# A float32 output projection becomes three float32r products, and moves one step later

## The chip, the cores and the metric

The kernel runs on one core of a Trainium2 chip. The metric is the device time of one execution in microseconds (us); lower is better. TensorE is PE in the profile, VectorE is DVE, ScalarE is ACT, GpSimd is POOL, SyncE (which issues the DMAs) is SP. The change touches only how one small matrix product is fed and when it runs.

## The reference, cut to what matters

Four attention layers follow each other on `x` (2048 x 256) with a context of 1601 x 512. Layers 0, 2 and 3 ("wide": 16 heads of 64) compute

```
q = x @ Wq;  k = ctx @ Wk;  v = ctx @ Wv          # 16 heads of 64
probs = softmax(q @ k.T / 8 + column bias)        # 2048 x 1601 per head
out = probs @ v                                   # 2048 x 1024, heads side by side
x = out @ Wo + bo + x                             # Wo: 1024 x 256
```

Layer 1 has 16 heads of 16 and an RMS norm; the change leaves it alone. The change is in `out @ Wo`: the product of the normalised attention output with `Wo`, added to the residual.

## The kernel before, in words

**Heads and steps.** A wide head is cut into 7 steps (`STEPS`) of two key tiles of 128 (the last has one). In a step the PE first runs 8 units, then multiplies the two tiles of exponentials with `V` (`values`, the L968 rows, float32, into banks OA and OB). A unit is one 128 x 512 score tile as two float32r products (`scores`, L957 and L958, into one of three ST banks) and one or two 400-wide score tiles for the row maximum of the next head (`s_tile`, L938, into one of three SS banks). ACT turns each ST bank into exponentials `P` (`exps`). DVE takes the maximum of each SS bank (`s_max`).

**Row sums.** The 13 tiles of exponentials of a head are added up in `acc`: tiles 0 to 2 on DVE (`add`, the first as 0 + 1, L1520, at the end of step 0; the second, L1526, at the end of step 1), tiles 3 to 12 on POOL (L838, two instructions a tile). POOL's first add of a head waits for DVE's second one, and its last adds of a head run into step 0 of the next head. In a layer's last head POOL has tiles 3 and 4 only, and DVE the others up to tile 10. Between its adds for tiles 7 to 10 POOL does four divisions (`divide`, L817), which write the normalised output of the head before into `On`.

**Output projection.** Two heads make a pair: `On` is 128 x 2048 (two heads of 64 rows), and `Wo`'s part of a pair is 128 x 256. A pair is projected in 8 items (`output`, L1003): item i gives 128 output columns by 512 rows of x; j = i // 2 says which 512 columns of `On` it reads. An item is one float32 product, which the trace shows as two MATMUL records. It takes an SS bank out of the same ring of three that `s_tile` uses (`wait_ring`: the bank must have been drained), and DVE adds it to the residual (`add_output`, L1546, or L1543 for a layer's first pair). `o_item` places the items: in steps 0 and 1 of odd heads from head 3 on, in every second unit. So 7 pairs of each layer go out inside heads 3, 5, ..., 15, and the eighth pair after the last head (`end`). `wo` has two buffers, loaded by SP at the end of odd heads.

**What sets the order.** Every engine runs a list written out in the program, in order. Semaphores with constant targets couple the lists. Instructions behind a waiting one wait too. The order of SS banks comes from `ring_order`, which PE, DVE and ACT all follow.

**Names the change touches.** `o_item`, `output`, `load_wo` and its calls in SP's `head`, `q_phase` and `group_layer`, the allocation of `On`, `wo` and `sel`, and the `head` functions of POOL, ACT and DVE.

Of the kernel before, what the change touches and what calls it, by code (L numbers as in the profile page):

```python
# [207 lines left out]
def attention_layers(nc, a):  # L208
    with ExitStack() as ctx:
# [15 lines left out]
        sel = at("sel", [128, 128], o + 1024)  # L225
# [46 lines left out]
        On = at("On", [128, NQ], o)  # L272
        o += 8192
# [4 lines left out]
        R = at("R", [128, 2, 512], o + 8192)  # L278
        o += 12288
        wo = [at(f"wo{b}", [128, C], o + 1024 * b) for b in range(2)]  # L280
        o += 2048

# [79 lines left out]
        d_wq, d_wo, d_m = sem("d_wq"), [sem(f"d_wo{b}") for b in range(2)], sem("d_m")  # L362
# [100 lines left out]
        def r_spread(H):  # L463

            return 128 * (H + 1 - (H + 1) // HEADS)

# [7 lines left out]
        def _(sp):  # L474
# [131 lines left out]
            def load_wo(n):  # L606
                sp.dma_start(wo[n % 2][:, :], a["wo"][n, :, :]).then_inc(d_wo[n % 2], 16)
# [15 lines left out]
            def q_phase(l):  # L623
# [38 lines left out]
                if l == 0:  # L662
                    load_v(1)
                    for n in range(2):
                        load_wo(n)
                if l == 2:
                    sp.wait_ge(pe_o, 8 * n0)
                    load_wo(n0 + 1)
# [64 lines left out]
            def group_layer():  # L733
# [10 lines left out]
                for h in range(HEADS):  # L744
# [12 lines left out]
                    if h == HEADS - 3:  # L757
# [3 lines left out]
                        for n in range(PAIRS, PAIRS + 2):  # L761
                            load_v(n)
                            load_wo(n)
# [30 lines left out]
        def _(gp):  # L794
# [24 lines left out]

            def head(H):  # L820
                first = adds_before(pool_tiles, H)
                for t in range(3, KT):
# [7 lines left out]
                    for c in range(2):  # L830
# [7 lines left out]
                        gp.tensor_tensor(out, out, P[0:k, slot(H, t), q, :], ALU.add).then_inc(pool_a, 1)  # L838

# [35 lines left out]
        def _(pe):  # L875
# [120 lines left out]
            def output(n, i):  # L996
                at, ct, j = RING_AT["o", n, i], i % CT, i // CT
                if i == 0:
                    pe.wait_ge(d_wo[n % 2], 16 * (n // 2 + 1))
# [3 lines left out]
                pe.matmul(SS[at % 3][:, :], wo[n % 2][:, ct * 128:(ct + 1) * 128], On[:, j * 512:(j + 1) * 512],  # L1003
# [31 lines left out]
            def head(l, h):  # L1035
                H = l * HEADS + h
                for g in range(STEPS):
                    for u, (on, t, j) in enumerate(units(h, g)):
# [3 lines left out]
                        if o_item(h, g, u) is not None:  # L1042
                            output(l * PAIRS + (h - 3) // 2, o_item(h, g, u))
# [11 lines left out]
            def end(l):  # L1055
                for i in range(8):
                    output(l * PAIRS + PAIRS - 1, i)
# [124 lines left out]
        def _(act):  # L1182
# [102 lines left out]

            def take_z(H):
# [36 lines left out]
            def head(l, h):  # L1323
                H = l * HEADS + h
                for g in range(STEPS):
                    if takes_sums(h, g - 1):
                        take_z(H - 1)
                    for on, t, j in units(h, g):
                        if j == 0:
                            exps(H + on, t)  # L1330
# [425 lines left out]
```

## Time and profile before

| | |
|---|---|
| time, median of 3 runs | 4620.56 us (4617.27 to 4621.11) |
| profiled execution | 4619.93 us |
| its span, first to last instruction | 4618.1 us |
| PE busy | 4523.6 us (98%) |
| DVE busy | 2989.6 us (65%) |
| POOL busy | 2674.4 us (58%) |
| ACT busy | 2262.0 us (49%) |
| granted PE clock, mean of the span | 0.987 of full speed |

The span is what the profile covers; 1.8 us of the execution's own time lie around it. A matmul's reported duration overlaps its neighbours, so the cost of one is read from the start of one row to the start of the next. A timeline row has start, duration, engine, line, operation, output and inputs, the count of merged instructions, and in brackets the idle time before it with its releaser. Where a row stands for several instructions, its duration is from the first one's start to the last one's end.

### The profile page before, as it was taken

To read this page: it belongs to the slowest core of one execution; us is meant where nothing else is said; L and a number is where in the kernel's file an instruction comes from. 1 tells how busy PE (TensorE), PEld (TensorE's weight loads), DVE (VectorE), ACT (ScalarE), POOL (GpSimd) and SP (SyncE) were. 2 spreads that over 40 slices of the span, in tenths; PEclk is the share of its full clock that TensorE was granted. 3 is DMA by queue.
4 is the path that set the end of the run, shared out by engine and by line. 5 is a ranking of instruction groups with operands and counts; after the bars stand their busy time and mean duration, and the time that the engine had idled before them with its cause. 6 is when DMAs were issued, how large, how long until landed. Compare 5 with 4: busy or idle time off the path is not lost.

```text
span 4618.1 us, 56243 instructions
## 1 busy us (share of the span) xinstructions
PE 4523.6 (98%) x20489; PEld 2807.1 (61%) x20489; DVE 2989.6 (65%) x5016; ACT 2262.0 (49%) x4016; POOL 2674.4 (58%) x1281
## 2 busy tenths in 40 slices
PE   8999999999999979999999999999999999999999
PEld 7888865555556545555556555555556655565554
DVE  3321467667766678778746667766767667676766
ACT  3222454454445436666655444444455545454443
POOL 0000367797778611111036887788774877788775
PEclk9999999999999979999999999999999999999999
DMA  4555832221222021011233221222216212222220
GB/s 151 178 188 163 289 79 64 66 68 45 66 64 52 12 39 16 12 15 16 58 109 111 67 67 45 64 68 52 52 46 221 63 39 64 64 68 54 58 48 28
DMA packets 124629, 349.64 MB, mean 76 GB/s; under 512 B 28085, under 2 KB 46005, under 8 KB 113338
## 3 DMA queue, kind: packets, MB, share of 16 engines
q1 hardware_dynamic: 124352, 346.04, 28.4%
q8 instruction: 162, 2.65, 0.3%
q14 instruction: 115, 0.94, 0.1%
HBM read 191.31 MB, written 120.31 MB: 67 GB/s over the span
## 4 chain that ended last, share of the span: by engine, by line
PE 95%; DVE 3%; DMA 1%; issue 1%; SPq 0%; ACT 0%; POOL 0%; DVEq 0%; ACTq 0%
PE ST L957 14%; PE SS L938 13%; PE ST L958 13%; PE OA L968 12%; PE OB L968 11%; PE ST L1090 5%; PE OA L1098 4%; PE SS L1003 4%; PE SS L1076 3%; PE OB L1076 1%; PE SS L977 1%; PE ST L1021 1%; PE ST L1022 1%; PE ST L1023 1%; DVE mpart L1599 1%; PE SS L925 1%
## 5 line engine op out<-in xcount | busy, mean ns | idle before, releaser
L838 POOL TENSOR_TENSOR acc<-acc,P 128x1024 f32<-128x1024 f32 x912 | 2203.2, 2448 | 598.4 <-DVE acc L1526 585.3
L1277 ACT ACTIVATE P<-ST 128x512 f32<-128x512 f32 (+1 forms) x2496 | 1465.4, 598 | 1305.4 <-PE ST L958 1169.8
L1499 DVE TENSOR_REDUCE mpart<-SS 128x1 f32<-128x400 f32 (+1 forms) x3072 | 1627.8, 569 | 676.2 <-PE SS L938 600.4
L938 PE MATMUL SS<-KS,QS 68*128 68x400 f32 (+1 forms) x3072 | 1037.9, 371 | 11.1 <-DMA QS<-stq 8.3
L957 PE MATMUL ST<-QX,KX 128*128 128x512 f32 (+1 forms) x2496 | 1032.9, 414 | 3.6 <-DMA QS<-mrow 2.0
L958 PE MATMUL ST<-QS,KS 69*128 69x512 f32 (+1 forms) x2496 | 989.0, 396 | 0.0
L938 PEld LDWEIGHTS SS<-KS,QS 68*128 68x128 f32 x3072 | 583.9, 190 | 222.6 <-DVE mpart L1499 33.5
L957 PEld LDWEIGHTS ST<-QX,KX 128*128 128x128 f32 (+1 forms) x2496 | 463.0, 185 | 389.2 <-issue 287.6
L968 PE MATMUL OA<-P,Vp 128*64 128x512 f32 (+1 forms) x2496 | 658.3, 606 | 0.0
L968 PE MATMUL OB<-P,Vp 128*64 128x512 f32 (+1 forms) x2496 | 641.3, 592 | 0.0
L1359 ACT ACTIVATE PG<-ST 128x512 f32<-128x512 f32 (+1 forms) x832 | 426.2, 616 | 213.3 <-PE ST L1090 213.0
L958 PEld LDWEIGHTS ST<-QS,KS 69*128 69x128 f32 (+1 forms) x2496 | 464.4, 186 | 14.7 <-issue 5.8
L847 POOL TENSOR_TENSOR On<-Oraw,Z 32x512 f32<-32x512 f32 x64 | 81.7, 1277 | 663.6 <-ACT Z L1184 660.0
L1599 DVE TENSOR_REDUCE mpart<-SS 128x1 f32<-128x400 f32 (+1 forms) x768 | 396.2, 563 | 83.0 <-PE SS L1076 83.0
L865 POOL TENSOR_TENSOR stq<-stw,stq 128x512 fp32r<-128x512 f32 x96 | 123.1, 1289 | 521.4 <-ACT stw L1184 519.7
L968 PEld LDWEIGHTS OB<-P,Vp 128*64 128x64 f32 (+1 forms) x2496 | 179.1, 137 | 356.6 <-issue 356.6
L968 PEld LDWEIGHTS OA<-P,Vp 128*64 128x64 f32 (+1 forms) x2496 | 149.3, 136 | 268.0 <-issue 181.8
L817 POOL TENSOR_TENSOR On<-Oraw,R 64x512 f32<-64x512 f32 x192 | 252.5, 1315 | 91.4 <-issue 40.2
L1546 DVE TENSOR_TENSOR xacc<-SS,xacc 128x512 f32<-128x512 f32 x168 | 115.7, 690 | 174.4 <-PE SS L1003 174.4
L1003 PE MATMUL SS<-On,wo 128*128 128x512 f32 x384 | 197.9, 605 | 9.0 <-issue 9.0
L1098 PE MATMUL OA<-PG,Vg 128*32 128x512 f32 (+1 forms) x1664 | 201.5, 599 | 0.0
L1526 DVE TENSOR_TENSOR acc<-acc,P 128x1024 f32<-128x1024 f32 x132 | 172.1, 1351 | 21.0 <-POOL acc L838 14.0
(240 smaller groups left out, 4206.4 us busy)
## 6 DMA issues: line engine op xcount, KB each, us to landing
q_parts<-stq SPq DMA_DIRECT2D x96, 512.0 KB, 5.4
QX<-q_parts SPq DMA_DIRECT2D x96, 512.0 KB, 11.3
KX<-k_parts SPq DMA_DIRECT2D x48, 801.0 KB, 9.2
QS<-q_parts SPq DMA_DIRECT2D x45, 512.0 KB
R<-R SPq DMA_DIRECT2D x360, 64.0 KB, 2.0
v_tiles<-sv SPq DMA_DIRECT2D x24, 832.0 KB, 6.4
Vp<-v_tiles SPq DMA_DIRECT2D x24, 832.0 KB, 7.2
k_parts<-skh SPq DMA_DIRECT2D x48, 400.5 KB, 4.9
```

What stands on the lines that cost most here:

```text
L817: gp.tensor_tensor(On[64 * e:64 * e + 64, j * 512:(j + 1) * 512], Oraw[r, c, :], R[r, c, :], ALU.mult)\
L838: gp.tensor_tensor(out, out, P[0:k, slot(H, t), q, :], ALU.add).then_inc(pool_a, 1)
L938: pe.matmul(SS[at % 3][:, 0:w], QS[H % 3][0:SROWS, qt * 128:(qt + 1) * 128], KS[H % 3][0:SROWS, o:o + w], start=True, stop=True).then_inc( ...
L957: pe.matmul(bank, KX[H % 2][:, t * 128:t * 128 + k], QX[H % 2][:, q], start=True, stop=False)
L958: pe.matmul(bank, KS[H % 3][0:MXROW + 1, t * 128:t * 128 + k], QS[H % 3][0:MXROW + 1, q], start=False, stop=True).then_inc(pe_st, 1)
L968: last = pe.matmul(OAB[j // 2][r:r + 64, :], Vp[n % 2][0:k, t, 64 * e:64 * e + 64], P[0:k, slot(H, t), j, :], start=t == 0, stop=t == KT - 1)
L1003: pe.matmul(SS[at % 3][:, :], wo[n % 2][:, ct * 128:(ct + 1) * 128], On[:, j * 512:(j + 1) * 512], start=True, stop=True).then_inc(pe_o, 1)
L1098: last = pe.matmul(OA[j * QD:j * QD + QD, :], Vg[0:k, t, g * QD:g * QD + QD], PG[slot(h, t) * JQ + j][0:k, :], start=t == 0, stop=t == KT - 1)
L1277: act.activation(P[0:k, slot(H, t), j, :], ST[n % 3][0:k, :], ACT.Exp, scale=SCALE).then_inc(act_p, 1)
L1359: act.activation(PG[slot(h, t) * JQ + j][0:k, :], ST[n % 3][0:k, :], ACT.Exp, scale=SCALE1).then_inc(gact_p, 1)
L1499: dve.tensor_reduce(mpart[H % 2][:, i // len(KCH), c:c + 1], SS[RING_AT["s", H, i] % 3][:, 0:w], AX.X, ALU.max).then_inc(dve_ss, 1)
L1599: dve.tensor_reduce(mpart[h % 2][:, i // len(KCH), c:c + 1], GS[GRING_AT["s", h, i] % 4][:, 0:w], AX.X, ALU.max).then_inc(gdve_ss, 1)
```

## The change

Inside the heads the float32 product becomes three float32r products that sum into one bank: hi weights by hi output, hi weights by lo output, lo weights by hi output. The last pair of a layer keeps the float32 product (`last_output`). Four new kinds of instruction make the parts:

- ACT copies `wo` to `woh` (128 x 256) after step 4 of the even head in which a pair's division runs, and DVE subtracts to get `wol`, right behind the maximum of the next head;
- ACT copies `On` to `Onh` in four pieces of 128 x 512: j = 0, 1 at the end of that even head, j = 2, 3 after step 1 of the odd head that follows (`Onh` has room for two pieces);
- POOL subtracts to get `Onl` (in place of `On`): j = 0, 1 behind its last add of the even head, j = 2, 3 in front of its first add of the odd head;
- an item's PE wait is now for `wol` (item 0) and for its piece of `Onl` (items 0, 2, 4, 6).

The items move from steps 0 and 1 to steps 1 and 2. `wo` has one buffer, and SP loads it behind the spreading of the reciprocals of the odd head instead of at its end. `sel`, used in layer 1 only, moves into an unused part of `R`.

```diff
 def o_item(h, g, u):
-    if h % 2 == 1 and h >= 3 and g < 2 and u % 2 == 0:
-        return 4 * g + u // 2
+    if h % 2 == 1 and h >= 3 and 1 <= g < 3 and u % 2 == 0:
+        return 4 * (g - 1) + u // 2
     return None
+def pair_ended(l, h):
+    return l * PAIRS + (h - 2) // 2 if h % 2 == 0 and h >= 2 else None
+def pair_going_out(l, h):
+    return l * PAIRS + (h - 3) // 2 if h % 2 == 1 and h >= 3 else None
...
# SP, head(l, h)
                 if h > 0:
                     spread(H - 1)
+                if pair_going_out(l, h) is not None:
+                    sp.wait_ge(pe_o, 8 * (pair_going_out(l, h) + 1))
+                    load_wo(pair_going_out(l, h) + 1)
...
-                if h % 2 == 1 and h >= 3 and H + 2 < end:
-                    sp.wait_ge(pe_o, 8 * (H // 2))
-                    load_wo(H // 2 + 1)
...
# POOL
+            def output_lo(n, j):
+                q = slice(j * 512, (j + 1) * 512)
+                gp.wait_ge(act_onh, 4 * split_before(n) + j + 1)
+                gp.tensor_tensor(Onl[:, q], On[:, q], words(Onh[:, j % 2, :]), ALU.subtract).then_inc(pool_onl, 1)
             def head(H):
+                if pair_going_out(l, h) is not None:
+                    for j in range(2, JQ):
+                        output_lo(pair_going_out(l, h), j)
                 for t in range(3, KT):
...
+                if pair_ended(l, h) is not None:
+                    for j in range(2):
+                        output_lo(pair_ended(l, h), j)
...
# PE, output(n, i)
                 if i == 0:
-                    pe.wait_ge(d_wo[n % 2], 16 * (n // 2 + 1))
+                    pe.wait_ge(dve_wol, split_before(n) + 1)
+                if ct == 0:
+                    pe.wait_ge(pool_onl, 4 * split_before(n) + j + 1)
+                wait_ring(pe, at)
+                pe.matmul(SS[at % 3][:, :], woh[:, w], Onh[:, j % 2, :], start=True, stop=False)
+                pe.matmul(SS[at % 3][:, :], woh[:, w], Onl[:, q], start=False, stop=False)
+                pe.matmul(SS[at % 3][:, :], wol[:, w], Onh[:, j % 2, :], start=False, stop=True).then_inc(pe_o, 1)
...
# ACT
+            def output_hi(n, j):
+                act.wait_ge(pool_on, 4 * (2 * n + 1) + j + 1)
+                wait(act, pe_o, 8 * n + 2 * j - 2)
+                copy(Onh[:, j % 2, :], On[:, j * 512:(j + 1) * 512]).then_inc(act_onh, 1)
+            def weights_hi(n):
+                act.wait_ge(d_wo, 16 * (n + 1))
+                copy(woh[:, :], wo[:, :]).then_inc(act_woh, 1)
...
# DVE
+            def weights_lo(n):
+                dve.wait_ge(act_woh, split_before(n) + 1)
+                dve.tensor_tensor(wol[:, :], wo[:, :], words(woh[:, :]), ALU.subtract).then_inc(dve_wol, 1)
...
+                    if g == 4 and pair_ended(l, h) is not None:
+                        weights_lo(pair_ended(l, h))
```

On POOL, at the turn from head 2 to head 3 of the first layer (`acc` is one head's sum, `Oraw` the raw output that is divided), the program before has these rows:

```order
L838 TENSOR_TENSOR acc_112<-acc_112,P 128x1024 x4
L838 TENSOR_TENSOR acc_112<-acc_112,P 65x1024 x2
L838 TENSOR_TENSOR acc_113<-acc_113,P 128x1024 x8
L817 TENSOR_TENSOR On<-Oraw,R 64x512
L838 TENSOR_TENSOR acc_113<-acc_113,P 128x1024 x2
```

The changed program has at the same place, on POOL:

```order
L867 TENSOR_TENSOR acc_111<-acc_111,P 128x1024 x4
L867 TENSOR_TENSOR acc_111<-acc_111,P 65x1024 x2
L844 TENSOR_TENSOR Onl<-On,Onh 128x512 x4
L867 TENSOR_TENSOR acc_112<-acc_112,P 128x1024 x8
L838 TENSOR_TENSOR On<-Oraw,R 64x512
```

The four subtractions stand between the last add of one head (65 rows high) and the first of the next; two of them belong to the one head and two to the other.

On DVE, in steps 0 and 1 of the same head 3 (`mpart<-SS` are row maxima, `xacc` the residual), the program before has:

```order
L1543 SCALAR_TENSOR_TENSOR xacc<-SS,bo,xacc 128x512
L1499 TENSOR_REDUCE mpart_52<-SS 128x1 x2
L1520 TENSOR_TENSOR acc_113<-P 128x1024 x2
L1543 SCALAR_TENSOR_TENSOR xacc<-SS,bo,xacc 128x512
L1499 TENSOR_REDUCE mpart_52<-SS 128x1 x3
```

The changed program has around the same adds on DVE, from the end of head 2 on:

```order
L1566 TENSOR_REDUCE negm<-mpart_52 128x16
L1591 TENSOR_TENSOR wol<-wo,woh 128x256
L1571 CAST mrow<-SS 16x128
L1560 TENSOR_REDUCE mpart_51<-SS 128x1 x24
L1581 TENSOR_TENSOR acc_112<-P 128x1024 x2
L1608 SCALAR_TENSOR_TENSOR xacc<-SS,bo,xacc 128x512
L1560 TENSOR_REDUCE mpart_51<-SS 128x1 x3
```

No item is left in front of DVE's first two adds of the odd head (`acc<-P`), and `wol` stands in front of the row of maxima.

On PE, behind the V products of head 2's last step (L1000 in the changed program, step 0's are the 128x512 rows of OA and OB), the changed program's first item reads:

```order
L989 MATMUL ST<-QX_68,KX_75 128x512
L990 MATMUL ST<-QS_64,KS_69 128x512
L1036 MATMUL SS<-Onh,woh 128x512
L1037 MATMUL SS<-Onl,woh 128x512
L1038 MATMUL SS<-Onh,wol 128x512
L970 MATMUL SS<-KS_70,QS_65 128x402
```

The three products stand where one L1003 row stood, behind the score tile of a unit.

## Rows read from the trace of the kernel before

**Rows 1.** The page: busy share of PE, and the chain that ended last.
```profile
PE 4523.6 (98%) x20489; PEld 2807.1 (61%) x20489; DVE 2989.6 (65%) x5016; ACT 2262.0 (49%) x4016; POOL 2674.4 (58%) x1281
...
PE 95%; DVE 3%; DMA 1%; issue 1%; SPq 0%; ACT 0%; POOL 0%; DVEq 0%; ACTq 0%
```

**Rows 2.** Timeline of PE, one unit with an item and one without, head 5.
```profile
903.10 1.02 PE L1003 MATMUL SS<-On,wo 128*128 128x512 f32 x2
...
904.14 0.39 PE L957 MATMUL ST<-QX,KX 128*128 128x512 f32 x1
...
904.61 0.35 PE L938 MATMUL SS<-KS,QS 68*128 68x400 f32 x1
904.79 0.39 PE L957 MATMUL ST<-QX,KX 128*128 128x512 f32 x1
```

**Rows 3.** Timeline of PE, three float32r products of 512 columns, V projection.
```profile
449.71 0.40 PE L925 MATMUL ST<-wvh,ch 128*128 128x512 f32 x1
...
450.41 0.39 PE L925 MATMUL ST<-wvh,ch 128*128 128x512 f32 x1
```

**Rows 4.** Timeline of PE, first layer: starts of steps in heads 5 and 6.
```profile
899.97 0.50 PE L957 MATMUL ST<-QX,KX 128*128 128x512 f32 x1
...
913.19 0.51 PE L957 MATMUL ST<-QX,KX 128*128 128x512 f32 x1
...
913.77 1.02 PE L1003 MATMUL SS<-On,wo 128*128 128x512 f32 x2
...
969.63 0.50 PE L957 MATMUL ST<-QX,KX 128*128 128x512 f32 x1
...
979.01 0.50 PE L957 MATMUL ST<-QX,KX 128*128 128x512 f32 x1
```

**Rows 5.** Timeline of POOL, its last add before head 5's own.
```profile
906.23 2.37 POOL L838 TENSOR_TENSOR acc<-acc,P 65x1024 f32<-65x1024 f32 x1
```

**Rows 6.** Timelines of POOL and DVE, their adds in step 0 of head 6.
```profile
973.93 5.70 POOL L838 TENSOR_TENSOR acc<-acc,P 65x1024 f32<-65x1024 f32 x2
...
976.03 1.39 DVE L1520 TENSOR_TENSOR acc<-P 128x1024 f32<-128x1024 f32 x1
...
977.34 3.37 DVE L1520 TENSOR_TENSOR acc<-P 128x1024 f32<-128x1024 f32 x1
```

**Rows 7.** Timelines of POOL and DVE, divisions beside adds, second wide layer's last head.
```profile
3471.57 2.05 POOL L817 TENSOR_TENSOR On<-Oraw,R 64x512 f32<-64x512 f32 x1 [0.17 <-POOL On L817]
3473.78 2.05 POOL L817 TENSOR_TENSOR On<-Oraw,R 64x512 f32<-64x512 f32 x1 [0.17 <-POOL On L817]
...
3472.40 2.29 DVE L1526 TENSOR_TENSOR acc<-acc,P 128x1024 f32<-128x1024 f32 x1
```

**Rows 8.** All instructions by line: POOL's subtraction of 128 x 512.
```profile
L865 POOL TENSOR_TENSOR stq<-stw,stq 128x512 fp32r<-128x512 f32 x96 | 123.1, 1289 | 521.4 <-ACT stw L1184 519.7
```

**Rows 9.** Timelines of PE, POOL and DVE, head 15 of the first layer.
```profile
1557.14 0.50 PE L957 MATMUL ST<-QX,KX 128*128 128x512 f32 x1
...
1568.11 0.50 PE L957 MATMUL ST<-QX,KX 128*128 128x512 f32 x1
...
1610.58 1.02 PE L989 MATMUL SS<-acc,ones 128*64 128x512 f32 x2
...
1554.13 15.00 POOL L838 TENSOR_TENSOR acc<-acc,P 128x1024 f32<-128x1024 f32 x6
...
1564.77 5.44 DVE L1520 TENSOR_TENSOR acc<-P 128x1024 f32<-128x1024 f32 x2
...
1592.71 15.71 DVE L1526 TENSOR_TENSOR acc<-acc,P 128x1024 f32<-128x1024 f32 x10
```

**Rows 10.** Busy time and granted clock by stretch (PEclk: third from the end); PE timeline.
```profile
203.00:209.00 6.00, 3.56 (x10) 2.60 (x9) 4.94 (x6) 1.84 (x4) 0.00 (x0) 0.73 0.97 318
279.00:285.00 6.00, 3.56 (x16) 2.79 (x16) 2.15 (x4) 2.11 (x5) 0.00 (x0) 1.00 0.81 266
...
572.00:577.00 5.00, 2.98 (x13) 1.78 (x12) 0.00 (x0) 3.03 (x7) 2.84 (x3) 1.00 1.05 408
...
205.89 0.80 PE L925 MATMUL SS<-wvh,ch 128*128 128x512 f32 x1 [2.44 <-DVE wvl L1424]
```

More of the change, by code:

```diff
@@ L272, in attention_layers @@
         On = at("On", [128, NQ], o)
+        Onl = at("Onl", [128, NQ], o, F32R)
         o += 8192
@@ L278, in attention_layers @@
         R = at("R", [128, 2, 512], o + 8192)
+        sel = at("sel", [128, 128], o + 8192 + 1024)
         o += 12288
-        wo = [at(f"wo{b}", [128, C], o + 1024 * b) for b in range(2)]
+        wo = at("wo", [128, C], o)
+        wol = at("wol", [128, C], o, F32R)
+        woh = at("woh", [128, C], o + 1024, F32R)
         o += 2048
+        Onh = at("Onh", [128, 2, 512], o, F32R)
+        o += 4096
         o = main
@@ L359, in attention_layers @@
         dve_bias, dve_tok, dve_ext = sem("dve_bias"), sem("dve_tok"), sem("dve_ext")
-        d_wq, d_wo, d_m = sem("d_wq"), [sem(f"d_wo{b}") for b in range(2)], sem("d_m")
+        d_wq, d_wo, d_m = sem("d_wq"), sem("d_wo"), sem("d_m")
+        act_woh, dve_wol, act_onh, pool_onl = sem("act_woh"), sem("dve_wol"), sem("act_onh"), sem("pool_onl")
         d_s = [sem(f"d_s{b}") for b in range(3)]
@@ L465, in r_spread, with split_before @@
             return 128 * (H + 1 - (H + 1) // HEADS)
+        def split_before(n):
+            return n - n // PAIRS
         def q_stored(l, q):
@@ L663, in q_phase @@
                     load_v(1)
-                    for n in range(2):
-                        load_wo(n)
+                    load_wo(0)
                 if l == 2:
                     sp.wait_ge(pe_o, 8 * n0)
-                    load_wo(n0 + 1)
+                    load_wo(n0)
             def head(l, h):
@@ L762, in group_layer @@
                             load_v(n)
-                            load_wo(n)
+                        load_wo(PAIRS)
                     sp.wait_ge(gpe_st, (h + 1) * HU)
@@ L1056, in end @@
                 for i in range(8):
-                    output(l * PAIRS + PAIRS - 1, i)
+                    last_output(l * PAIRS + PAIRS - 1, i)
             def group_project(rnd, j):
@@ L1330, in head @@
                             exps(H + on, t)
+                    if g == 1 and pair_going_out(l, h) is not None:
+                        for j in range(2, JQ):
+                            output_hi(pair_going_out(l, h), j)
+                    if g == 4 and pair_ended(l, h) is not None:
+                        weights_hi(pair_ended(l, h))
+                if pair_ended(l, h) is not None:
+                    for j in range(2):
+                        output_hi(pair_ended(l, h), j)
                 if h == 0:
@@ L1580, in head @@
                         reciprocals(H - 1)
+                    if g == 4 and pair_ended(l, h) is not None:
+                        weights_lo(pair_ended(l, h))
             def end(l):
```

17 lines of the change are left out of this document (11 added, 6 removed).

## The prediction

> **What bounds the kernel now.** I read the page first: PE is busy for 98% of the span and carries 95% of the chain that ended last [rows 1]. So any time taken off the PE's list inside the heads is time off the span, as long as PE never has to wait; and any new wait of PE is paid in full. Then I read PE's timeline in a head with items and in one without, always from start to start. An item's rows begin at 903.10 and the next unit's first product at 904.14; of these 1.04 us the 400-wide tile in between takes 0.18 (904.61 to 904.79), so one float32 item costs PE 0.86 us [rows 2]. A step without items lasts 9.38 us (969.63 to 979.01), one with four items 13.22 (899.97 to 913.19) [rows 4]: 3.84 for four items, of which 3.44 are the items themselves and 0.4 are short waits for an SS bank. Last I read POOL and DVE around the turn of the heads, because the changed items wait for POOL. All times there are from T, the start of a head's first score product behind the V products of the head before.
>
> **The product itself.** 168 items lie in the heads (7 pairs x 8 items x 3 layers). Three float32r products of 512 columns take 0.70 us from start to start (449.71 to 450.41, each with its own weight load) [rows 3]. That is 0.16 less than 0.86, and 168 x 0.16 = 26.9 us off. The bounds: 0.14 to 0.17 an item, 23 to 29 us. The section "TensorE Precision Notes" of the page FP8 and Floating Point Precision of the Trainium skill says that true float32 takes four passes and reduced float32 one; by that ratio three products would cost three quarters of 0.86, and the sum would be some 9 us lower. The rows show 0.70 and not 0.645, so I stay with 0.16. PE's four fewer items in step 0 and four more in step 2 cancel but for the waits priced below.
>
> **The wait that the change adds.** Item 0 of an odd head waits for Onl's first piece, and the whole of PE's list stands behind it: scores, maxima, V products, and with them ACT and DVE. When is that piece ready?
>
> Item 0 is now in step 1. Step 0 has lost its items and lasts 9.38 like that of an even head; the item comes 0.58 later (913.19 to 913.77) [rows 4]. So PE is there at T + 9.96.
>
> POOL's last add of the head before runs from 906.23 to 908.60, that is T + 6.26 to T + 8.63 [rows 5], and `output_lo` stands behind it. A POOL subtraction of 128 x 512 takes 1.29 us [rows 8]. With nothing else the piece would be ready at T + 9.9, just in time. Two things come in between.
>
> First, DVE. In head 5 DVE's two first adds came behind step 0's items. Without them DVE does what it does in even heads: its first add starts at 976.03, T + 6.40, and it collides with POOL. In head 6 two POOL adds take 5.70 us and not 2 x 2.37, the second DVE add takes 3.37 and ends at T + 11.08 [rows 6, 5]. Each waits for the other's whole instruction. In [rows 7] the two engines take turns: a POOL instruction of 512 columns starts every 2.21 us, of which DVE's 1024 columns fill 1.07 (from the end of POOL's at 3473.62 to DVE's own end at 3474.69) and POOL's own work 1.14.
>
> Second, the new `wol` subtraction on DVE in step 4 of the even head, 128 x 256. One 1024-column DVE add held POOL up by 5.70 - 4.74 = 0.96 us [rows 5, 6], so a quarter of the columns should cost it 0.24 to 0.3. POOL has no idle time from there to the end of the head's adds, so the shift stays. The trace has no such small DVE instruction beside POOL; the bounds are 0 (it does not collide) and 0.96 (it does like a whole add). I take 0.27. The section "Who interferes with whom" of the page SBUF — State Buffer of the Trainium skill says that a tensor_tensor with both inputs in SBUF contends with GpSimd's reads; `wo` and `woh` both lie in SBUF, so by that the shift is there and not zero. It adds to the chance of this order and to no term.
>
> With 0.27 POOL's last add would start at T + 6.53, behind DVE's first at T + 6.40, so DVE goes first and both run as in head 6: POOL's add ends about T + 10.0, DVE's second add T + 11.08, and only then `output_lo` runs, for 1.14. The piece is there at T + 12.2, PE starts at T + 12.3: a wait of 2.35 us. Heads 3 to 13 of each layer are 6 x 3 = 18: +42.3 us. While PE waits, DVE catches up, so about 0.2 of bank waits go: -3.6.
>
> The other new waits are covered. Pieces j = 2, 3: ACT copies them (0.6 each) and POOL subtracts during the V products of step 1 (3.6 us) and PE needs the third only behind the row sums and a unit, some 2 us after it is ready. `wol` on DVE and `woh` on ACT lie under the V products of step 4. ACT's two copies at a head's end fit into its idle time before it drains OA. SP's load of `wo` waits for items that are done before the reciprocals it has just spread. If one of these covers fails, it costs at most the 0.6 to 1.3 us of the copy or subtraction for each of 21 pairs, up to 27 us.
>
> POOL in an odd head starts its adds about 3.2 us later, counted from the end of step 1, but the head then has 2.8 + 0.4 more to go in step 2 and no DVE add is in its way. It comes to the next even head about 0.9 us earlier, which lets DVE finish there before PE needs a bank: 0 to 0.3 us a head, I take 4 us off.
>
> **The last head of a layer.** It has no maxima to compute, so its steps are short. With four items one lasts 1568.11 - 1557.14 = 10.97; without, 7.54. PE is at item 0 at T + 8.1. POOL is busy till 1569.13, T + 12.0, and this with one of DVE's adds in its way [rows 9]. Now nothing stands before DVE's first adds, so both come early and both delay POOL: 12.0 + 0.96 + 0.27, then 1.2 for the subtraction: T + 14.4. PE waits 6.3 us; in the second wide layer POOL is 1.1 later. Together +20 us. Behind it DVE's adds end at 1608.42, and PE's sums begin at 1610.58 [rows 9]; both move by 5 to 6 us, so 2.2 us of room are left to lose about 1.
>
> **The clock.** PE will be idle for about 2.2 us (2.35 less the tail of the product before). A gap of 2.44 us was followed by a fall to 1.2 GHz for part of the stretch (granted 0.73) and by none the next time (1.00); of five such gaps four fell, and one of about 2.0 at 572 did not [rows 10]. A fall here cost 6.00 x 0.27 = 1.6 us. I count 9 of 18: +15 us, bounds 0 and 29. The 6 us waits in the last heads will bring a fall each, about 2 us: +6.
>
> **Sum.** -26.9 + 42.3 - 3.6 - 4 + 20 + 15 + 6 = +49 us. The profiled execution took 4619.9 (span 4618.1 and 1.8 around it), 0.6 under the median of 4620.56. 4619.9 + 49 = 4669 us, about 1.1% slower.
>
> **Rivals.**
> - *POOL keeps its place before DVE.* If the `wol` subtraction delays POOL by less than 0.14, POOL's last add starts first, the two engines take turns from there, and the piece is ready at about T + 11.0. The wait is 1.15 us, too short for the clock to fall. 18 x 1.15 = 21, less 27, less 4, plus 20 + 6: +16, 4636 us. For it: in [rows 5] POOL is only 0.14 ahead of DVE. Against it: POOL is full from step 4 on.
> - *No collision, so faster.* If `output_lo` does not have to queue behind DVE's add, the piece is ready at T + 9.9, PE does not wait, and only the last heads pay: -27 - 4 + 17 = -14, 4606 us. It decides at T + 9.96: every tenth later costs 1.8 us over the 18 heads, and 0.8 us later eats the gain. For it: POOL alone would be just in time. Against it: every even head shows the collision at the very place where the odd heads will now be.
> - *Every gap brings the clock down*, or the sums of the last head come late: 4669 + 14 + 6 = 4689 us.
> - *It pays what it gains.* The products save less (0.14) and the first rival's order holds in some heads and no collision in others: within 9 us of before.
>
> **Chances and range.** The forecast 0.60 (own range 4650 to 4688), POOL first 0.17, no collision 0.10, every gap 0.07, even 0.06. About 0.2%, 9 us, is what a measurement of this kernel can tell from no change. Slower by more: 0.83 (the forecast, every gap, and nearly all of POOL first); within: 0.08; faster: 0.09. The range that leaves out 2 in 10 runs from 4622 to 4690.
>
> **What will show it.** In the changed profile PE's rows should have one idle time of about 2.2 us in step 1 of heads 3 to 13, released by POOL's `Onl`, 18 times, and 6 to 7.5 us in the three last heads; an item should take 0.70 from start to start; DVE's first add of an odd head should start about T + 6.4 and its second end about T + 11; step 0 of odd heads should last 9.4. The granted clock should show short falls inside the layers, where before it had none. The forecast is wrong if PE's waits for `Onl` come to under 30 us in all, if they are released by ACT's copies and not by POOL, or if PE waits behind the moved items in step 2.

## The result

The changed kernel takes 4639.4 us, median of 6 runs (4635.0 to 4641.9), against 4620.6 for the kernel before (6 runs, 4617.3 to 4622.3): ratio 1.0041, 95% interval 1.0028 to 1.0054. It is slower by 19 us. The forecast said slower by 49: the direction was right, and its largest term was not. The profiled execution took 4641.9 us with a span of 4640.1, 22.0 more than the span before.

The page after, its busy time and its chain, beside [rows 1]:

```profile
PE 4505.8 (97%) x20657; PEld 2843.7 (61%) x20657; DVE 3106.2 (67%) x5037; ACT 2309.6 (50%) x4121; POOL 2825.3 (61%) x1365
...
PE 94%; DVE 3%; issue 1%; DMA 1%; SPq 1%; ACT 0%; POOL 0%; DVEq 0%; ACTq 0%
```

PE works 17.8 us less and the span is 22.0 longer: 40 us more in which PE stands still. The view of the waits (engine, line, what it waited for: us in total, times, longest) holds nearly all of it in one row:

```profile
PE SS L1036 <- issue: 38.7, 21, 6.2
```

L1036 is the first product of an item, and the 21 waits are the 21 pairs: item 0 stands still each time. The releaser is not named ("issue"); the timelines name it below. The same view of the kernel before has only three waits for its item line, at the layers' ends, and these are still there.

PE's timeline in head 5, the starts of steps 0 and 1, the row sums at the end of step 1 and the start of step 3, beside [rows 4]:

```profile
896.50 0.50 PE L989 MATMUL ST<-QX,KX 128*128 128x512 f32 x1
...
905.85 0.50 PE L989 MATMUL ST<-QX,KX 128*128 128x512 f32 x1
...
919.75 1.06 PE L1009 MATMUL SS<-acc,ones 128*32 128x512 f32 x8
...
933.32 0.51 PE L989 MATMUL ST<-QX,KX 128*128 128x512 f32 x1
```

Step 0 has become 9.35 us (13.22 before), step 1 is 13.90 where it was 13.22, step 2 takes 13.57 where it was 10.37. Over the three steps the head stands where it stood: what the product saves, the wait in step 1 takes.

PE's timeline at item 0 of the same head. The number in brackets is the idle time ahead of an instruction:

```profile
906.19 0.39 PE L990 MATMUL ST<-QS,KS 69*128 69x512 f32 x1
907.67 0.47 PE L1036 MATMUL SS<-Onh,woh 128*128 128x512 f32 x1 [1.09 <-issue]
907.97 0.40 PE L1037 MATMUL SS<-Onl,woh 128*128 128x512 f32 x1
```

The timelines of POOL and DVE there, beside [rows 5, 6]. T is 896.50:

```profile
900.66 2.40 POOL L867 TENSOR_TENSOR acc<-acc,P 65x1024 f32<-65x1024 f32 x1
...
903.01 2.36 POOL L867 TENSOR_TENSOR acc<-acc,P 65x1024 f32<-65x1024 f32 x1
905.32 4.48 POOL L844 TENSOR_TENSOR Onl<-On,Onh 128x512 fp32r<-128x512 f32 x2
...
902.87 3.58 DVE L1581 TENSOR_TENSOR acc<-P 128x1024 f32<-128x1024 f32 x1
```

POOL's last add starts at T + 6.51 and DVE's first at T + 6.37. The forecast had T + 6.53 and T + 6.40. But DVE, which is there first, does not go first: its add takes 3.58 us and POOL's takes 2.36, undisturbed. When both are there, POOL's add before the last is still running (to 903.06), so the question is who goes when that one ends. In head 6 of the kernel before, with the same order of starts and also beside a running add, it was DVE: its add took 1.39 and the two POOL adds 5.70 [rows 6]. Here it is POOL. So POOL is free for the piece at T + 8.87, the two lined-up pieces take turns with DVE's two adds (2.24 each), and the first is ready at T + 11.1. PE comes back at T + 11.17.

Head by head, from the start of the last V product of one head to that of the next: the 18 odd heads 3 to 13 last 3.0 us longer in all, the even heads 2.8 shorter, and the three last heads 21.9 longer (61.1, 61.2 and 60.2 against 53.5). The sum is the 22.0 of the span, to 0.1. Nearly the whole net loss is in three of 48 heads; in the 18 odd ones the waits took what the product gave. In the first of these, beside [rows 9], the timelines of PE, POOL and DVE, then stretches with busy times and the granted clock (third number from the end):

```profile
1561.39 0.39 PE L990 MATMUL ST<-QS,KS 69*128 69x512 f32 x1
1568.03 0.77 PE L1036 MATMUL SS<-Onh,woh 128*128 128x512 f32 x1 [6.25 <-issue]
...
1550.78 15.93 POOL L867 TENSOR_TENSOR acc<-acc,P 128x1024 f32<-128x1024 f32 x6
1566.67 2.49 POOL L844 TENSOR_TENSOR Onl<-On,Onh 128x512 fp32r<-128x512 f32 x2
...
1551.02 6.55 DVE L1581 TENSOR_TENSOR acc<-P 128x1024 f32<-128x1024 f32 x2 [8.55 <-ACT P L1321]
...
1566.00:1573.00 7.00, 4.97 (x12) 3.96 (x13) 1.02 (x2) 1.19 (x2) 3.16 (x3) 0.51 0.01 2
1573.00:1580.00 7.00, 7.00 (x31) 3.54 (x30) 5.00 (x5) 3.87 (x7) 2.27 (x2) 1.00 0.00 0
```

PE waits 6.25 us and comes back at 1.2 GHz (0.51 from 1566 to 1573, so for some 5 us of work). The forecast had a wait of 6.3 and a fall in each last head.

### The profile page after: what moved, and what is told of

It reads as the page before. It is cut to its first block, busy times and chain, and to the rows that moved or that the text cites. A ratio compares the mean times of both kernels' runs of the same rounds, so it can differ in the third digit from the quotient of the medians.

```text
span 4640.1 us, 56871 instructions
## 1 busy us (share of the span) xinstructions
PE 4505.8 (97%) x20657; PEld 2843.7 (61%) x20657; DVE 3106.2 (67%) x5037; ACT 2309.6 (50%) x4121; POOL 2825.3 (61%) x1365
## 4 chain that ended last, share of the span: by engine, by line
PE 94%; DVE 3%; issue 1%; DMA 1%; SPq 1%; ACT 0%; POOL 0%; DVEq 0%; ACTq 0%
PE ST L989 14%; PE SS L970 13%; PE ST L990 12%; PE OA L1000 12%; PE OB L1000 11%; PE ST L1134 5%; PE OA L1142 4%; PE SS L1120 3%; PE OB L1120 1%; PE SS L1036 1%; PE SS L1009 1%; PE SS L1037 1%; PE SS L1038 1%; PE ST L1065 1%; PE ST L1066 1%
## 5 line engine op out<-in xcount | busy, mean ns | idle before, releaser
L867 POOL TENSOR_TENSOR acc<-acc,P 128x1024 f32<-128x1024 f32 x912 | 2180.0, 2421 | 297.3 <-DVE acc L1587 284.1
L970 PE MATMUL SS<-KS,QS 68*128 68x400 f32 (+1 forms) x3072 | 977.2, 352 | 11.5 <-DMA QS<-stq 8.7
L1000 PE MATMUL OA<-P,Vp 128*64 128x512 f32 (+1 forms) x2496 | 658.3, 606 | 0.0
L1000 PE MATMUL OB<-P,Vp 128*64 128x512 f32 (+1 forms) x2496 | 641.3, 592 | 0.0
L1000 PEld LDWEIGHTS OB<-P,Vp 128*64 128x64 f32 (+1 forms) x2496 | 179.1, 137 | 356.6 <-issue 356.6
L1000 PEld LDWEIGHTS OA<-P,Vp 128*64 128x64 f32 (+1 forms) x2496 | 149.3, 136 | 265.9 <-issue 178.4
L844 POOL TENSOR_TENSOR Onl<-On,Onh 128x512 fp32r<-128x512 f32 x84 | 176.2, 2116 | 162.8 <-ACT Onh L1228 162.8
L1581 DVE TENSOR_TENSOR acc<-P 128x1024 f32<-128x1024 f32 x96 | 231.4, 2450 | 25.7 <-ACT P L1321 25.7
```

What stands on the lines that cost most here:

```text
L970: pe.matmul(SS[at % 3][:, 0:w], QS[H % 3][0:SROWS, qt * 128:(qt + 1) * 128], KS[H % 3][0:SROWS, o:o + w], start=True, stop=True).then_inc( ...
L1000: last = pe.matmul(OAB[j // 2][r:r + 64, :], Vp[n % 2][0:k, t, 64 * e:64 * e + 64], P[0:k, slot(H, t), j, :], start=t == 0, stop=t == KT - 1)
```

## The experiments

All ratios are against runs of the kernel before on the same chip, with their 95% interval. Sums over heads come from the starts of V products in the profiled executions.

### The product alone

The changed kernel with the items back in steps 0 and 1, three float32r products, no low pieces (the edit against the changed kernel, cut). One product is added up three times, so only the time of this kernel means something.

```diff
-                pe.matmul(..., woh[:, w], Onh[:, j % 2, :], start=True, stop=False)
-                pe.matmul(..., woh[:, w], Onl[:, q], start=False, stop=False)
-                pe.matmul(..., wol[:, w], Onh[:, j % 2, :], start=False, stop=True)
+                pe.matmul(..., woh[:, w], Onr[:, q], start=True, stop=False)
+                pe.matmul(..., woh[:, w], Onr[:, q], start=False, stop=False)
+                pe.matmul(..., woh[:, w], Onr[:, q], start=False, stop=True)
```

> The items stand in steps 0 and 1 as in the kernel before, as three float32r products, but all three read the rounded weights and the rounded output (POOL's division writes float32r), so the lo parts are left out, and with them ACT's copies of On and POOL's and DVE's subtractions. Theory (products gain, waits lose): nothing new to wait for, 168 x 0.16 = 27 us under the kernel before, about 4593 us, an item 0.70 us from start to start. Rival (the product itself gains little beside SS bank waits): within 10 us of before, 4610 to 4620.

4592.5 us, ratio 0.9941 (0.9928 to 0.9953), 27.4 us less by their spans; the odd heads give 23.5 of it and the last heads 4.0. The first term of the sum is right.

### The moved items alone

```diff
-    if h % 2 == 1 and h >= 3 and g < 2 and u % 2 == 0:
+    if h % 2 == 1 and h >= 3 and 1 <= g < 3 and u % 2 == 0:
```

> The kernel before with the eight items of an odd head moved to its second and third steps, as one float32 product each. Theory A (the wait in the second step comes from GpSimd's pieces, which take VectorE's turn): step 0 gives 3.87 us, step 2 takes 3.87, step 1 waits no more than 0.3 us for a bank; 4618 to 4624. Rival B (the move alone puts the items where the banks come free late): step 1 waits 1.2 us in each of 18 heads, +22 us, 4640.

4616.4 us, ratio 0.9998 (0.9989 to 1.0007). The odd heads change by +0.1 us in all, the last by +0.7, the even ones by -4.4. Moving costs nothing. In 16 of the 18 odd heads DVE's first add goes second here as well, but because POOL's add is there first, by 0.05 us (POOL, then DVE, head 5):

```profile
903.46 2.35 POOL L838 TENSOR_TENSOR acc<-acc,P 65x1024 f32<-65x1024 f32 x1
...
903.51 3.38 DVE L1520 TENSOR_TENSOR acc<-P 128x1024 f32<-128x1024 f32 x1
```

### Nothing lined up behind the last add

The changed kernel with one wait in front of the first two low pieces. It is for POOL's own last add, which the order of POOL's list already puts in front of them.

```diff
+                    gp.wait_ge(pool_a, adds_before(pool_tiles, H + 1))
                     for j in range(2):
                         output_lo(pair_ended(l, h), j)
```

> The changed kernel, and POOL waits for its own last add before the two lo pieces behind it, so that no further instruction stands ready behind that add. Theory A (DVE's first add lost the turn only because more POOL work was already lined up): the collision goes as in even heads, DVE's first add takes about 1.3 us instead of 3.6, POOL's last add about 3.3 instead of 2.35, the first lo piece is ready about 1.1 us later, PE's wait in step 1 of heads 3 to 13 rises from 1.3 to about 2.4 us: +18 us or more, 4657 to 4675 us. Theory B (the order has nothing to do with what is lined up): POOL only pays the wait of about 0.1 us, DVE still waits 3.6 us, 4639 to 4645 us.

4684.3 us, ratio 1.0133 (1.0117 to 1.0148): one wait costs about 45 us. POOL, DVE and PE in head 5 (T is 898.25), and two stretches:

```profile
904.72 3.34 POOL L867 TENSOR_TENSOR acc<-acc,P 65x1024 f32<-65x1024 f32 x1
...
904.62 1.22 DVE L1582 TENSOR_TENSOR acc<-P 128x1024 f32<-128x1024 f32 x1
...
910.37 0.47 PE L1037 MATMUL SS<-Onh,woh 128*128 128x512 f32 x1 [2.04 <-issue]
...
904.00:910.00 6.00, 4.33 (x19) 1.36 (x18) 5.15 (x4) 1.14 (x2) 5.92 (x3) 1.00 0.00 0
910.00:920.00 10.00, 9.63 (x36) 7.89 (x36) 6.57 (x12) 3.59 (x6) 1.52 (x2) 0.83 0.01 2
```

DVE gets its turn (1.22 us), the piece comes a us later, PE idles 2.04 and then works at 1.2 GHz for part of the next ten us (0.83 in the mean). This is the forecast's course of things, and its time is above the forecast's 4669. So the forecast failed not at when things start but at who goes.

### Is it the lined-up work? Four runs in the kernel before

If work behind the add decides who goes at the add, it must do so in the even heads of the kernel before too. There two POOL subtractions whose results nothing uses were put behind POOL's last add, in front of each of 21 even heads.

```diff
+                if H % HEADS % 2 == 1 and H % HEADS + 1 < HEADS:
...
+                    for b in range(2):
...
+                        gp.tensor_tensor(idle[b][:, :], held, held, ALU.subtract)...
```

> The kernel before, with two GpSimd subtractions of 128x500 (operands and targets that nothing else waits for) lined up behind GpSimd's last add in front of each even head of the wide layers (21 heads). Nothing that they write is used. Theory A (ScalarE's and GpSimd's products aside, VectorE loses its turn at the adds when GpSimd has more work lined up): in these heads VectorE's first add of tile 1 takes about 3.6 us instead of 1.27, its second ends at 12.8 us after the head's start instead of 11.5, and step 1 grows from 9.38 to about 10.7: 21 x 1.2 = +25 us, 4643, and more (up to 4690) where the TensorE clock then falls. Rival B (the turn goes by who is issued first; GpSimd's pieces don't matter for it): VectorE's first add stays at 1.27 us, and the time stays at 4618 to 4622.

4619.3 us, ratio 1.0004 (0.9995 to 1.0013): nothing. The theory as I had put it falls. But these subtractions read one operand twice; the real pieces read two. So next, subtractions in the pieces' own form:

```diff
-                        gp.tensor_tensor(idle[b][:, :], held, held, ALU.subtract)...
+                        gp.wait_ge(act_o, 2 * H)
+                        gp.tensor_tensor(idle[b][:, :], held[:, 0:504], held[:, 512:1016], ALU.subtract)...
```

> The kernel before with two GpSimd subtractions of the pieces' form (two different operands, 128x504, F32R written, a met wait on ScalarE's semaphore at each) behind GpSimd's last add in front of each even head. Their results are used by nothing. Theory A in its narrow form (what follows the last add matters, by its form or its met waits, since plain 128x500 subtractions changed nothing): VectorE's first add takes 3.4 to 3.6 us and its second ends at 12.7, step 1 grows by about 1.2 us in 21 heads, 4640. Rival E (it is something else in the changed kernel's odd heads): 1.3 us stays, 4618.

4661.6 us, ratio 1.0087 (1.0072 to 1.0103). The even heads grow by 44.5 us, all in step 1; DVE's first add takes 3.35 to 4.3 us in each of the 21 (in the kernel before, 1.3 to 2.3 in 19 of them), and in six of them the clock fell as well. Two more runs split this form: two operands with plain float32 targets and no met wait at the second, then one operand with F32R targets and met waits.

```diff
-... idle[b][:, :], held, held, ALU.subtract)
+... idle[b][:, :], held[:, 0:500], held[:, 512:1012], ALU.subtract)
...
-... idle[b][:, :], held[:, 0:504], held[:, 512:1016], ALU.subtract)
+... idle[b][:, :], held[:, 0:504], held[:, 0:504], ALU.subtract)
```

> As the run with two plain subtractions of 128x500 behind GpSimd's last add in front of each even head (which changed nothing), but of two different operands instead of one read twice; still plain float32 targets and no wait at the second. Theory O (work lined up takes VectorE's turn if it reads two different operands, as an add does): VectorE's first add 3.6 us, even heads +44 us, 4655 to 4662. Rival F (the F32R target or the met waits take the turn): 1.3 us and 4618.

> As the run with two subtractions in the pieces' form (F32R target, met waits), but with one operand read twice. Theory O: VectorE gets its turn (first add 1.3 us), 4618. Rival F: 3.6 us, 4655 to 4662.

Two operands: 4662.6 us, ratio 1.0099 (1.0082 to 1.0116). One operand: 4617.9, ratio 0.9999 (0.9989 to 1.0009). In both forms it is the second operand. In the first of the four runs (one operand), POOL and DVE in head 6:

```profile
973.40 3.34 POOL L841 TENSOR_TENSOR acc<-acc,P 65x1024 f32<-65x1024 f32 x1
976.71 2.00 POOL L846 TENSOR_TENSOR idle<-Vg 128x500 f32<-128x500 f32 x1
...
973.16 1.36 DVE L1528 TENSOR_TENSOR acc<-P 128x1024 f32<-128x1024 f32 x1
```

The same rows in the run with two operands and plain float32 targets:

```profile
982.62 2.35 POOL L841 TENSOR_TENSOR acc<-acc,P 65x1024 f32<-65x1024 f32 x1
984.92 2.25 POOL L846 TENSOR_TENSOR idle<-Vg 128x500 f32<-128x500 f32 x1
...
982.38 3.68 DVE L1528 TENSOR_TENSOR acc<-P 128x1024 f32<-128x1024 f32 x1
```

Both times DVE's add starts 0.24 us ahead of POOL's. What differs is an instruction that POOL reaches 2.3 us later.

### Which partitions? Two runs

POOL's last add covers 65 partitions, the pieces 128. The two-operand subtractions on partitions 0 to 63, then on 96 to 127 alone (the second edit is shown; in both, POOL's first add of the head also waits for them):

```diff
-... idle[b][:, :], held[:, 0:500], held[:, 512:1012], ...
+... idle[b][96:128, :], held[96:128, 0:500], held[96:128, 512:1012], ...
```

> The two-operand subtractions lined up in front of each even head, on partitions 0 to 63 alone, which GpSimd's last add (65 partitions) covers too; GpSimd's first add of the head waits for them. Theory P (GpSimd's upper part, which the 65-partition add leaves free, starts the lined-up work early and keeps the reads): VectorE gets its turn, first add 1.3 us, 4618. Rival Q (any lined-up work with two operands takes the turn): first add 3.6 us, 4655 to 4662.

> The same on partitions 96 to 127 alone, which GpSimd's last add does not cover. Theory P: VectorE loses its turn, its first add takes 2.5 us or more, 4640 to 4662. Rival Q: 3.6 us as well. If VectorE keeps its turn here and not in the run on the lower partitions, both fall.

4618.6 us, ratio 1.0000 (0.9988 to 1.0011), and 4620.5, ratio 1.0005 (0.9994 to 1.0016). DVE keeps its turn in both, in the same 19 heads as in the kernel before; on the upper partitions, in head 6:

```profile
974.15 1.25 DVE L1530 TENSOR_TENSOR acc<-P 128x1024 f32<-128x1024 f32 x1
```

So neither half does what the whole does. My theory of the partitions that the add leaves free explains the first run and fails at the second; "any lined-up work with two operands" fails at both. Why the width matters stays open.

### Is it the form of the wait?

The run that gave DVE its turn had given the piece a second wait. Here it has one too, but one that is always met.

```diff
+                    gp.wait_ge(pool_a, adds_before(pool_tiles, H + 1) - 8)
```

> The changed kernel in which GpSimd's first low piece also waits for its own adds up to the eighth before the last, which are done some 17 us earlier: the same form of instruction (two waits) as in the run in which the piece waited for the last add, but a wait that is always met. Theory A (VectorE loses its turn when a piece that could start is lined up behind the last add): no change, VectorE's first add stays at 3.6 us, 4636 to 4642. Rival D (the second wait as such makes the gap in which VectorE gets its turn): as with the wait for the last add, VectorE's first add 1.3 us, step 1 at 16 us or more, 4684.

4641.1 us, ratio 1.0047 (1.0032 to 1.0062), as the changed kernel, and DVE's first add stays at 3.6 us (4.3 in one head). The form does nothing.

### Without the weights' subtraction

The third product repeats the first, so the result counts that one twice; here too only the time means something.

```diff
-                pe.matmul(SS[at % 3][:, :], wol[:, w], Onh[:, j % 2, :], ...)
+                pe.matmul(SS[at % 3][:, :], woh[:, w], Onh[:, j % 2, :], ...)
```

> The changed kernel without VectorE's subtraction of the weights; the third product takes the rounded weights once more, so the weights' low part is left out of the result. Theory A: GpSimd's adds end 0.24 us earlier in the odd heads, VectorE still loses its turn (the pieces are still lined up), so the wait in the second step goes from 1.15 to about 0.9 us: 18 x 0.24 = -4.3 us, 4635. Rival C (the 0.24 us decide whether VectorE gets its turn): VectorE's first add falls back to 1.27 us or the wait goes altogether, -20 us or more.

4636.5 us, ratio 1.0038 (1.0026 to 1.0051), span 5.3 us shorter than that of the changed kernel. In a typical odd head POOL's last add starts 0.17 to 0.21 us earlier, so the 128x256 subtraction does delay POOL, by a little less than the 0.27 that the forecast took. The 18 odd heads give 2.4 us and the last heads 1.3. DVE is now behind POOL by right (T + 6.37 against T + 6.32 in head 5), and the wait goes from 1.09 to 0.90 us, by no more than the shift: whether the subtraction is there decides nothing about the turn.

### The last heads

First with the float32 items of the kernel before in their steps 0 and 1 (`is_split` is false in a layer's last two heads; the edit is cut), then with float32r items one step later.

```diff
+    f = 1 if is_split(h) else 0
-    if h % 2 == 1 and h >= 3 and 1 <= g < 3 and u % 2 == 0:
+    if h % 2 == 1 and h >= 3 and f <= g < f + 2 and u % 2 == 0:
```

> The changed kernel in which a layer's last head keeps the float32 items of the kernel before in its first two steps, without pieces. Theory: the 21.9 us that the three last heads gained go, the other heads stay: 4639.4 - 21.9 = 4617.5. Rival (the odd heads of the changed kernel are what made it slower, and the last heads are even with before): 4635 or more.

4617.7 us, ratio 1.0000 (0.9990 to 1.0009). The last heads are within 0.1 us of before and the loss of the change is gone, though not one us is gained: the odd heads are 3.7 us longer than before, the even ones 3.3 shorter.

> The changed kernel, and only in the last head of each layer the items stand in steps 2 and 3, with ACT's second copies behind step 2 and POOL's second subtractions behind its adds for tile 4. Theory (the whole loss of the change sits in the three last heads, where PE waits for the first lo piece): those heads go from 61 us to about 53 each, 22 to 25 us under the changed kernel, about 4616 us. Rival (there DVE's and POOL's adds become the end of the layer): the gain is under 10 us, over 4629 us.

4627.7 us, ratio 1.0017 (1.0008 to 1.0026): not all came back: the last heads are still 8.1 us longer than before. The wait went from step 1 to step 3. PE, then DVE, there in the first layer:

```profile
1588.54 0.39 PE L996 MATMUL ST<-QS,KS 69*128 69x512 f32 x1
1590.90 0.50 PE L1042 MATMUL SS<-Onh,woh 128*128 128x512 f32 x1 [1.97 <-DVE xacc L1617]
...
1580.29 6.75 DVE L1593 TENSOR_TENSOR acc<-acc,P 128x1024 f32<-128x1024 f32 x2 [1.27 <-POOL acc L873]
1586.96 3.34 DVE L1602 RECIPROCAL R<-Zs 128x512 f32<-128x512 f32 x1
1590.22 2.41 DVE L1617 TENSOR_TENSOR xacc<-SS,xacc 128x512 f32<-128x512 f32 x4
...
1580.29 4.52 DVE L1593 TENSOR_TENSOR acc<-acc,P 128x1024 f32<-128x1024 f32 x1 [1.27 <-POOL acc L873]
...
1582.46 1.27 POOL L850 TENSOR_TENSOR Onl<-On,Onh 128x512 fp32r<-128x512 f32 x1
```

The items need banks that DVE must empty, and DVE is in two adds, held up by POOL's pieces, and a reciprocal. I had asked only when the pieces are ready. The last two rows are the first of the two adds by itself and a piece: the add takes 4.52 us, because the piece, which starts 2.17 us after it, goes first (1.27, undisturbed), with another piece behind.

### All items later, and the version that beats both

Items of every odd head in steps 2 and 3, which I thought would take PE out of reach of the pieces:

> The items of all odd heads stand in steps 2 and 3, ACT's second copies behind step 2, POOL's second subtractions behind its adds for tile 4. Theory (the products gain 27 us, all of which the wait in step 1 and the last heads took): no PE wait for a lo piece is left, step 1 pays up to 0.8 us of SS bank waits because DVE's second add ends late; 4620 - 27 + 18 x 0.5 = about 4602, range 4594 to 4610 us. Rival (POOL, with 84 subtractions more, comes late for the tiles of the next head or for the divisions, and ACT and PE wait for it): 4615 us or more.

4677.0 us, ratio 1.0121 (1.0103 to 1.0138). A bad miss: the 18 odd heads are 52 us longer than before. Step 1 has no items now, yet lasts 10.7 to 15.6 us in the odd heads 3 to 13 and 16.7 in one; in 11 of the 18 the clock fell. PE's timeline in heads 5 and 11 of the first layer, and the stretch behind each:

```profile
911.58 0.45 PE L976 MATMUL SS<-KS,QS 68*128 68x400 f32 x1 [1.12 <-DVE mpart L1566]
...
1310.30 0.45 PE L976 MATMUL SS<-KS,QS 68*128 68x400 f32 x1 [1.13 <-DVE mpart L1566]
...
913.00:923.00 10.00, 10.00 (x49) 5.65 (x48) 6.84 (x11) 4.56 (x9) 5.64 (x3) 1.00 0.00 0
...
1312.00:1322.00 10.00, 10.00 (x29) 5.13 (x27) 5.46 (x8) 2.49 (x5) 3.23 (x2) 0.55 0.00 0
```

DVE, which lost its turn, ends its adds late and empties the banks late, and PE waits 1.1 us for a bank. In head 5 nothing more happens; in head 11, after the same wait, the clock falls to 1.2 GHz for about ten us. The remedy is to give DVE its turn. That hurt where PE waited for the piece; here PE comes for the pieces only some 7 us after both are ready (907.99 and 914.89 in head 5 of the next run).

```diff
+    f = 2 if is_split(h) else 0
...
+                    gp.wait_ge(dve_a, added_by(dve_tiles, H + 1, 1))
                     for j in range(2):
                         output_lo(pair_ended(l, h), j)
```

The last heads keep their float32 items.

> The changed kernel with the items in a head's third and fourth steps; GpSimd takes the first two low pieces only when VectorE's two adds of tile 1 are done, the last two between its own adds of tiles 4 and 5; a layer's last head keeps the float32 items of the kernel before, in its first two steps. Theory A (VectorE loses its turn only to work lined up behind GpSimd's last add; with that work held back its adds end at 11.5 us as in the even heads of the kernel before): steps 0 and 1 of the odd heads are 9.38 and 9.4 to 9.6 us, steps 2 and 3 13.55 and 12.6: 68.6 us against 69.7, 18 x -1.1 = -20 us, the even heads -4, the last heads 0: 4596. Rival B (items in the fourth step or late pieces cost banks whatever holds them back): step 1 stays at 10.7 us or more, 4620 to 4680.

4593.6 us, ratio 0.9949 (0.9936 to 0.9961), with its sibling below the fastest kernel here that does the full computation: 24 us less than before and 46 less than the change. Step 1 of an odd head is back at about 9.6, the odd heads give 18.4 us and the even ones 6.1. POOL and DVE in head 5:

```profile
900.97 3.34 POOL L873 TENSOR_TENSOR acc<-acc,P 65x1024 f32<-65x1024 f32 x1
905.47 2.52 POOL L850 TENSOR_TENSOR Onl<-On,Onh 128x512 fp32r<-128x512 f32 x2 [1.16 <-DVE acc L1590]
...
900.84 1.25 DVE L1590 TENSOR_TENSOR acc<-P 128x1024 f32<-128x1024 f32 x1
902.01 3.38 DVE L1590 TENSOR_TENSOR acc<-P 128x1024 f32<-128x1024 f32 x1
```

The same kernel without its one wait, and with the wait for POOL's own add in its place:

> The version that beats both kernels, without the one wait that holds the first two low pieces behind VectorE's adds of tile 1. Theory: VectorE loses its turn again, step 1 of the odd heads goes from 9.4 to 10.7 us where the clock stays up and to 14 to 15.6 where it falls, as with all items in steps 2 and 3: 18 x 1.2 = +22 us at least, with falls in half of the heads +60: 4616 to 4665, likeliest 4655. Rival (the late steps alone are what makes it fast, the wait does nothing): 4594.

> The version that beats both kernels, with its one wait changed: the first two pieces wait only for GpSimd's own last add, not for VectorE's adds. Theory A (it is enough that no piece is lined up behind the add when VectorE asks): VectorE's first add 1.3 us, its second ends at 11.5 beside the piece, step 1 stays at 9.4 to 9.6: 4594. Rival G (a piece beside VectorE's second add costs banks as well): VectorE's adds end later than 11.5 or step 1 grows by 0.3 us or more in 18 heads: 4600 or more.

Without: 4671.5 us, ratio 1.0116 (1.0093 to 1.0139). With POOL's own: 4594.5, ratio 0.9953 (0.9938 to 0.9967). The one wait is worth some 78 us, and for whom it waits does not matter; what matters is that no piece can start when DVE asks.

## Why the prediction was right in part, and wrong in its largest term

- *Product, -26.9.* Right: 27.4 measured alone. An item takes the 0.70 of [rows 3], not the 0.645 of the ratio of passes. (Of that ratio the section of the Trainium skill that the prediction names states the four passes; the one pass of reduced float32 is my reading of it.)
- *The shift by `wol`, 0.27.* Right within 0.1: POOL's last add starts at T + 6.51 where T + 6.53 was forecast, and 0.17 to 0.21 earlier without the subtraction.
- *The wait of the odd heads, 18 x 2.35.* This is the step that failed: "behind DVE's first at T + 6.40, so DVE goes first and both run as in head 6". The starts are as forecast, and POOL goes first all the same, because two pieces with two operands stand behind its add; the four runs in the kernel before show that this suffices. PE idles 1.1 us instead of 2.2: 21.1 us in the 18 heads, where 2.2 us each would be 39.6. I had taken the order of head 6 over to a place where POOL's queue holds something else. The Trainium skill, page SBUF — State Buffer, section "Who interferes with whom", says "Issue order, not op shape, decides who blocks". Here one order of starts, beside a running POOL add, gave both outcomes, by the shape of a later POOL instruction; the measurement decides.
- *The clock in odd heads, +15.* It hangs on the step above: with 1.1 to 1.4 us of idle it stayed up in 17 of the 18 heads, and fell in the one in which PE waited 2.2. Where PE did idle for 2.0 us or more, in the run with nothing lined up, it fell in 15 of 18, and the 18 heads came to +49 us against before instead of +3.
- *Vanished bank waits, -3.6.* They did not vanish: in head 5, step 2 spends 3.20 us on four items that cost 2.80, and step 1 has 0.64 left (13.90 less 9.37, 2.80 and 1.09), where a step with items had 0.4 before. In all, waits and clock cost the 18 heads 3.0 + 23.5 = 26.5 us, where 42.3 - 3.6 + 15 = 53.7 were forecast. That difference, 27.2, is the whole error of the forecast's 49 against the span's 22.0.
- *Even heads, -4.* 2.8 less measured; 4.4 with the items merely moved.
- *Last heads, +20 and +6.* Right in the sum and the cause, with luck in the parts: with their share of the product, 4.0, taken off, +22 was forecast and +21.9 came. The idle times are 6.25, 5.7 and 5.6 us, 17.6 where 20 was forecast: POOL was not later in the second wide layer but earlier. A clock fall came in each, and with what else there is the rest came to 8.3 where 6 was forecast.
- *The rival "POOL keeps its place before DVE"* gave 4636 us and a wait of 1.15, which is what came, but for a cause that is refuted: it asked for a shift under 0.14, and the shift was 0.17 or more. Its "too short for the clock to fall" held in this kernel; with all items later the clock fell in 10 of the 17 heads with 1.1 to 1.4 us of idle.
- *The covers.* PE waits for no other piece in step 2, as said.
- *The signs of being wrong.* None of the three came: the waits for `Onl` are 38.7 us, above the 30 named, but 17.6 of them lie in the last heads, so that sum could not show the error in the odd ones. What did show it is the end of DVE's second add: T + 12.15 in head 5, where about T + 11 was said.

## What to carry to other kernels

Where VectorE and GpSimd compete, look not only at who starts first but at what each has lined up behind: a wait that parts a GpSimd instruction from the work behind it can give VectorE its turn, or take TensorE's result away, and here cost about 45 us in one place and gave 78 in another. Move the work of a faster product to where its operands have been ready for long, and ask then what else in that step needs the engine that empties its banks. And price the short steps by themselves: three of 48 heads held the whole net loss.

## What the runs showed of the hardware

- A DVE add of 1024 columns that starts 0.1 to 0.3 us ahead of POOL's, while POOL's add before that one still runs, goes first (1.2 to 1.4 us, POOL's 3.34), unless two-operand POOL instructions over all 128 partitions follow POOL's add and are free to start. Then DVE waits it out (3.6 us), even where it started 1.26 us ahead: 4.68 us in head 3 of the second wide layer. With one operand read twice, or on partitions 0 to 63 or 96 to 127 alone, DVE keeps its turn. Why was not found.
- Being next in POOL's list is not enough. In head 15 of the changed kernel DVE's first add goes ahead of a POOL add over 128 partitions, though more such adds follow; each of those waits for the POOL add two places in front of it, and the pieces wait for nothing that is still open. And the turn is lost once: DVE's add goes ahead of the first piece, which takes 2.24 us in place of 1.27.

```profile
1551.02 3.22 DVE L1581 TENSOR_TENSOR acc<-P 128x1024 f32<-128x1024 f32 x1 [8.55 <-ACT P L1321]
...
1553.10 3.39 POOL L867 TENSOR_TENSOR acc<-acc,P 128x1024 f32<-128x1024 f32 x1
```

- One and the same idle time of PE, 1.12 and 1.13 us in one kernel, was followed by full clock in one head and by about ten us at 1.2 GHz in another. Over the heads of that kernel, 1.1 to 1.4 us was followed by a fall in 10 of 17; in the changed kernel in none of 17; in the run with nothing lined up, 2.0 us and more in 15 of 18.
- A DVE subtraction of 128x256 beside a full POOL costs POOL about 0.2 us.
